# Macaron layer (FFN, retention, FFN) on eight cores: VectorE's start written as alternating chains, first FFN of chunk 5 ahead of V 0, second FFN of chunk 8 held back to the end, Wo 2 and a second FFN exchanged in step 4

## What is computed

```python
def _L0_ffn_ref(x, weight, bias):            # weights and rows in blocks of 32
    xq, xs = _mx_quantize(x2)                # fp6 grid, scale = max|block| / 7.5
    wq, ws = _mx_quantize(w2)
    out = (xq * xs[..., None]) @ (wq * ws[..., None]).T + bias
def _retention(X, Wq, Wk, Wv):               # 8 heads of 128
    scores = jnp.einsum('bhnd,bhmd->bhnm', q, k) / np.sqrt(DH)
    ret = jnp.einsum('bhnm,bhmd->bhnd', scores * decay[None], v)
    ret = (ret - mean) * jax.lax.rsqrt(var + EPS)        # per head
# attention: silu(X @ W_G) * Y @ W_O, with X 2048 x 1024 on each core
x = x + 0.5 * _L0_ffn_ref(_layernorm(x), weight, bias)
x = x + _L0_attn_ref(_layernorm(x), Wq, Wk, Wv, W_G, W_O)
x = x + 0.5 * _L0_ffn_ref(_layernorm(x), weight, bias)
```

## Time and profile before

| | us |
|---|---|
| median of 3 runs (lowest, highest) | 485.18 (484.07, 485.69) |
| the profiled execution | 484.67 |
| span of its slowest core, from first to last instruction | 482.8 |
| spans of the eight cores | 479.5 to 482.8 |
| TensorE busy in the span | 432.3 (90%) |
| VectorE busy | 342.6 (71%) |
| GpSimd busy | 256.4 (53%) |
| ScalarE busy | 190.5 (39%) |

### The profile page before, as it was taken

The page is one execution under the profiler, slowest core; times in us unless marked ns, Lnnn a source line. Parts: engine busy times, 40 slices in busy tenths (PEclk is TensorE's granted clock), DMA queues, the critical chain, the costliest instruction groups (busy, mean ns, idle before and its releaser), DMA issues.

```text
span 482.8 us, 8182 instructions; the slowest of 8 cores (479.5 to 482.8 us)
## 1 busy us (share of the span) xinstructions
PE 432.3 (90%) x2410; PEld 215.5 (45%) x2456; DVE 342.6 (71%) x656; ACT 190.5 (39%) x270; POOL 256.4 (53%) x328
## 2 busy tenths in 40 slices
PE   0226799999998999999999999999999999999894
PEld 0113354545543535454545445454545454555442
DVE  3886866477888859687786868586947466756782
ACT  1547265236442071607061533426152534614400
POOL 0888765325477554655647464647451624436243
PEclk9999899999999999999999999999999999999999
DMA  7999999974363393635343533645340524233143
GB/s 200 309 182 182 189 157 183 155 116 87 89 110 67 94 208 92 110 67 143 75 133 67 153 68 88 88 88 88 87 81 12 107 45 85 47 67 65 44 153 131
DMA packets 99451, 54.47 MB, mean 113 GB/s; under 512 B 88784, under 2 KB 89040, under 8 KB 99408
## 3 DMA queue, kind: packets, MB, share of 16 engines
q1 hardware_dynamic: 93984, 43.43, 39.5%
q0 software_dynamic: 5280, 10.49, 14.9%
q10 hardware_dynamic: 144, 0.03, 0.0%
HBM read 34.28 MB, written 8.39 MB: 88 GB/s over the span
## 4 chain that ended last, share of the span: by engine, by line
PE 72%; DVE 12%; issue 6%; ACT 3%; DMA 3%; POOL 2%; SPq 1%; DVEq 1%; ACTq 0%; POOLq 0%
PE p L818 64%; DVE p L419 2%; DVE arena L434 2%; PE p L928 2%; DMA arena<-arena 2%; PE pstate L908 1%; PE p L859 1%; DVE arena L444 1%; DMA arena<-wf 1%; PE p L863 1%; PE p L847 1%; ACT arena L709 1%; ACT arena L681 1%; PE pstate L872 1%; DVE arena L522 1%
## 5 line engine op out<-in xcount | busy, mean ns | idle before, releaser
L818 PE MATMUL p<-arena 128*128 128x512 bf16 x1715 | 383.2, 379 | 8.1 <-ACT arena L709 2.7
L818 PEld LDWEIGHTS p<-arena 128*128 128x128 bf16 x1760 | 169.6, 98 | 206.8 <-issue 10.6
L434 DVE BATCH_NORM_STATS2 arena<-arena 128x6 f32<-128x512 f32 x96 | 66.5, 692 | 9.9 <-DVE arena L436 2.2
L669 ACT ACTIVATE arena<-arena 128x1024 bf16<-128x1024 f32 x16 | 19.9, 1243 | 129.1 <-POOL arena L1072 129.1
L1112 POOL TENSOR_TENSOR arena<-arena 128x1024 bf16<-128x1024 fp8e4 x16 | 34.3, 2144 | 46.9 <-DVE arena L449 46.9
L681 ACT ACTIVATE arena<-p,arena 128x128 bf16<-128x128 f32 x128 | 46.4, 473 | 19.2 <-POOL arena L1085 19.2
L444 DVE TENSOR_REDUCE arena<-arena 128x32 f32<-128x1024 f32 x29 | 35.3, 1216 | 19.3 <-ACT arena L660 10.8
L513 DVE TENSOR_TENSOR arena<-p,arena 128x1024 bf16<-128x1024 f32 x16 | 19.6, 1223 | 41.0 <-PE p L818 40.5
L908 PE MATMUL pstate<-arena 128*128 128x128 bf16 x168 | 16.4, 261 | 34.3 <-POOL arena L1048 27.5
L1105 POOL TENSOR_TENSOR arena<-arena 128x1024 bf16<-128x1024 fp8e4 x16 | 30.5, 1909 | 29.3 <-DVE arena L449 26.3
L449 DVE SCALAR_TENSOR_TENSOR arena<-arena 128x1024 fp8e4<-128x1024 f32 x29 | 37.3, 1285 | 3.4 <-DVE arena L448 0.5
(11 more groups left out here) (52 smaller groups left out, 397.1 us busy)
## 6 DMA issues: line engine op xcount, KB each, us to landing
arena<-x SPq DMA_DIRECT2D x16, 512.0 KB, 5.3
out<-arena SPq DMA_DIRECT2D x16, 512.0 KB, 2.8
arena<-wf SPq DMA_DIRECT2D x8, 512.0 KB, 11.5
arena<-wk POOLq DMA_DIRECT2D x2, 1024.0 KB, 19.9
arena<-wq POOLq DMA_DIRECT2D x2, 1024.0 KB, 31.5
arena<-wg POOLq DMA_DIRECT2D x2, 1024.0 KB, 40.0
arena<-wv POOLq DMA_DIRECT2D x2, 1024.0 KB, 41.2
arena<-wo POOLq DMA_DIRECT2D x2, 1024.0 KB, 34.0
```

What stands on the lines that cost most here:

```text
L434: step(e.bn_stats(bn_ln[:, n, 6 * half:6 * half + 6], x[:, 512 * half:512 * half + 512]))
L818: last = e.matmul(pair[:, half * 512:half * 512 + 512], lhs[:, kc, :], w[:, kc, half * 512:half * 512 + 512], start=(kc == 0), stop=(kc == ...
```

## The change

VectorE's first instructions are written as two chains that alternate: while one weight block or chunk waits for its own last result, an instruction of the next stands between. ScalarE loads its function table at once (`warm`) and takes some steps in another order; GpSimd issues four of its loads later and takes its small steps in another order. On TensorE `f1(5)` is taken ahead of `proj(0, "v")` instead of behind `ret(0)`; the first FFN of chunk 1 is cut in two halves; `proj(2, "v")` and `wo(0)` are exchanged; in step 4 `wo(2)` and `f2(1)` are exchanged. `f2(8)` leaves step 11 and joins the units behind `sc(15)`, where two units (chunks 11 and 14) are also cut in halves around a turn. The x loads of chunks 6 and 7 go behind `kt(1)`, `qt(1)` and the arrival of Wv.

```diff
-F2_IN = 9
+F2_IN = 8
...
-             ("g", 1, 1), ("v", 0, 0), ("sc", 0, 1), ("v", 1, 2), ("ret", 0, 1),
-             ("f1", 5, 0), ("k", 2, 2), ("q", 2, 0), ("sc", 1, 1), ("g", 2, 2),
-             ("ret", 1, 1), ("wo", 0, 0), ("v", 2, 2),
+             ("g", 1, 1), ("f1", 5, 0), ("v", 0, 2), ("sc", 0, 1), ("v", 1, 0),
+             ("ret", 0, 1), ("k", 2, 2), ("q", 2, 0), ("sc", 1, 1), ("g", 2, 2),
+             ("ret", 1, 1), ("v", 2, 0), ("wo", 0, 2),
...
+        if F2_IN + 3 <= i < LATE:
...
+        elif i == STEADY:
+            order += [("f1", i + 3, 0), ("sc", i - 1, 1), ("wo", i - 2, 2),
+                      ("ret", i - 1, 1), ("f2", i - 3, 0), ("k", i, 2), ("q", i, 0),
+                      ("g", i, 2), ("v", i, 1)]
...
-    late_home = {9: cols(o_xc1[0]), 10: cols(o_xc1[0] + 2048), 11: cols(o_xc1[1]),
+    late_home = {8: cols(o_xd1[0]), 9: cols(o_xc1[0]), 10: cols(o_xc1[0] + 2048), 11: cols(o_xc1[1]),
...
+            elif c == 8:
+                e.wait_ge(sem["tr_x10"], 16 * n_dma(14, X1_DMA, 2))
...
-        e.wait_ge(sem["t_k"], 2)
+        kt(1)
+        qt(1)
+        e.wait_ge(sem["ld_wv"], 32)
         x_first(6)
-        kt(1)
         x_first(7)
...
+        store(8)
...
+        def w_max(j):
             e.wait_ge(sem["ld_wf%d" % j], 16)
+            own.up(e.tensor_reduce(w_amax[j % 4].unsqueeze(2), b32(wst_sb[j]), AX, ALU.max,
+                                   apply_absolute_value=True))
+            at["w_max", j] = own.n
+        def w_scale(j):
             if j >= 4:
                 e.wait_ge(sem["g_wd"], j - 3)
+            e.wait_ge(sem["v_self"], at["w_max", j])
+            own.up(e.tensor_scalar(w_scl[j % 4], w_amax[j % 4], 0.5 * R7_5, 0.5 * FLOOR,
+                                   ALU.mult, ALU.max))
+            at["w_scale", j] = own.n
+        def w_recip(j):
+            e.wait_ge(sem["v_self"], at["w_scale", j])
+            own.up(e.reciprocal(w_rs[j % 4], w_scl[j % 4]))
+            at["w_recip", j] = own.n
+        def w_mul(j):
             if j >= 2:
                 e.wait_ge(sem["s_wy8"], j - 1)
+            e.wait_ge(sem["v_self"], at["w_recip", j])
+            e.scalar_tensor_tensor(b32(wy_sb[j % 2]), b32(wst_sb[j]), 0.5,
+                                   bc32(w_rs[j % 4]), ALU.mult, ALU.mult
+                                   ).then_inc(sem["v_wy"], 1)
...
-        wquant(0)
-        wquant(1)
-        st1(0)
-        for j in range(2, 6):
-            wquant(j)
-        q1(0)
-        wquant(6)
-        st1(1)
-        wquant(7)
-        q1(1)
-        st1(2)
-        q1(2)
+        w_max(0)
+        w_scale(0)
+        w_max(1)
+        w_recip(0)
+        w_scale(1)
+        w_mul(0)
+        x_st(0, 0)
+        w_recip(1)
+        x_st(0, 1)
+        w_mul(1)
+        w_max(2)
+        x_mean(0)
+        w_scale(2)
+        for j in range(3, 6):
+            w_max(j)
+            w_recip(j - 1)
+            w_scale(j)
+            w_mul(j - 1)
+        x_max(0)
+        w_recip(5)
+        x_scale(0)
+        w_mul(5)
+        w_max(6)
+        x_recip(0)
+        w_scale(6)
+        x_mul(0)
+        x_st(1, 0)
+        w_recip(6)
+        x_st(1, 1)
+        w_mul(6)
+        w_max(7)
+        x_mean(1)
+        w_scale(7)
+        x_st(2, 0)
+        w_recip(7)
+        w_mul(7)
+        x_max(1)
+        x_st(2, 1)
+        x_scale(1)
+        x_mean(2)
+        x_recip(1)
+        x_mul(1)
+        x_max(2)
+        x_scale(2)
+        x_recip(2)
+        x_mul(2)
...
         evV(3)
         ev2(0)
         st2(4)
-        for i in range(STEADY, NC):
+        mask(3)
+        ev1(7)
+        q1(8)
+        evO(2)
+        gn(3)
+        ev2(1)
+        st2(5)
+        st3(2)
+        st1(9)
+        q2(2)
+        zmul(3)
+        evV(4)
+        q1(9)
+        for i in range(STEADY + 1, NC):
...
-        for j in range(KC - 1):
+        e.wait_ge(sem["g_const"], 2)
+        e.activation(warm, nhalf, AF.Identity, bias=ntie)
+        wy8(0)
+        wy8(1)
+        xc1(0)
+        for j in range(2, 6):
             wy8(j)
-            if 2 <= j:
-                wcp(j - 2)
-            if j == 2:
-                xc1(0)
-            if j == 4:
-                e.wait_ge(sem["ld_bias"], 16)
-                e.activation(bias_sb, bias_sb, AF.Identity, scale=0.5
-                             ).then_inc(sem["s_bias"], 1)
-        xc1(1)
+            wcp(j - 2)
+        e.wait_ge(sem["ld_bias"], 16)
+        e.activation(bias_sb, bias_sb, AF.Identity, scale=0.5).then_inc(sem["s_bias"], 1)
+        wcp(4)
+        wy8(6)
         wcp(5)
         xcp(0)
+        xc1(1)
         wy8(7)
         wcp(6)
+        xc1(2)
         wcp(7)
-        xc1(2)
         xcp(1)
         xcp(2)
         tn(0)
...
         tn(4)
         for i in range(STEADY, NC):
             if i < LATE:
-                tn(i + 1)
+                if i > STEADY:
+                    tn(i + 1)
                 scopy(i - 1)
                 evK(i)
+                if i == STEADY:
+                    tn(i + 1)
                 xc2(i - 2)
...
+        def f2_half(c, half):
+            e.wait_ge(sem["tr_x2"], 16 * (c + 1))
+            pair = emptied("f2", c)
+            for kc in range(KC):
+                last = e.matmul(pair[:, half * 512:half * 512 + 512], xdt2_at(c)[:, kc, :],
+                                wdt_sb[:, kc, half * 512:half * 512 + 512],
+                                start=(kc == 0), stop=(kc == KC - 1),
+                                skip_group_check=True)
+            if half == 1:
+                last.then_inc(sem["t_f2"], 1)
...
-        f1(1)
+        f1_half(1, 0)
         xtr(2)
+        f1_half(1, 1)
         f1_half(2, 0)
...
+        xtr(5)
         proj(1, "g")
-        xtr(5)
         e.wait_ge(sem["s_t"], 3)
         turn("t2", t_sb)
+        f1(5)
         proj(0, "v")
         sc(0)
         proj(1, "v")
         ret(0)
-        f1(5)
         proj(2, "k")
         proj(2, "q")
         sc(1)
         proj(2, "g")
         ret(1)
+        proj(2, "v")
         wo(0)
-        proj(2, "v")
...
             if i < LATE:
                 f1(i + 3)
                 sc(i - 1)
-                if i < F2_IN + 3:
+                if STEADY < i < F2_IN + 3:
                     f2(i - 3)
                 else:
                     wo(i - 2)
                 ret(i - 1)
-                if i < F2_IN + 3:
+                if i == STEADY:
+                    f2(i - 3)
+                elif i < F2_IN + 3:
                     wo(i - 2)
                 proj(i, "k")
             else:
...
-        f2(9)
+        f2(8)
         ret(NC - 1)
         wo(NC - 2)
+        f2(9)
         f2(10)
-        f2(11)
         e.wait_ge(sem["s_Sc"], NC - 1)
         e.wait_ge(sem["v_z"], NC)
         turn("z%d" % Z_PE, z_sb)
+        f2_half(11, 0)
         wo(NC - 1)
+        f2_half(11, 1)
         f2(12)
         f2(13)
-        f2(14)
+        f2_half(14, 0)
         e.wait_ge(sem["g_xd2"], NC)
         turn("y%d" % X2_PE, xd2_sb)
+        f2_half(14, 1)
         f2(NC - 1)
...
-        cast_load("wg", 1)
         xd1(0)
         b1(0)
         wd(6)
-        cast_load("wv", 0)
         sm1(1)
         wd(7)
         xd1(1)
         sm1(2)
+        cast_load("wg", 1)
+        cast_load("wv", 0)
+        xd1(2)
         b1(1)
+        sm2(0)
         cast_load("wv", 1)
-        xd1(2)
-        sm2(0)
         b1(2)
         sm1(3)
         sm2(1)
+        xd1(3)
         cast_load("wo", 0)
-        xd1(3)
+        b1(3)
         cast_load("wo", 1)
-        b1(3)
         sm1(4)
         sm2(2)
+        sm1(5)
         b1(4)
         xd1(4)
-        sm1(5)
         b1(5)
         xd1(5)
...
```

More of the change, by code:

```diff
@@ L180, in build_program @@
     y82_sb = f8at(take(1024), D)
-    xd1_sb = [bfat(take(2048), D) for _ in range(2)]
+    o_xd1 = [take(2048) for _ in range(2)]
+    xd1_sb = [bfat(o, D) for o in o_xd1]
     o_xd2 = take(2048)
@@ new lines, in x_recip, with x_mul, x_st @@
+        def x_recip(c):
+            e.wait_ge(sem["v_self"], at["x_scale", c])
+            own.up(e.reciprocal(x_rs[c], q1_scl[c % 2]))
+            at["x_recip", c] = own.n
+        def x_mul(c):
+            e.wait_ge(sem["v_self"], at["x_recip", c])
+            e.scalar_tensor_tensor(b32(y81_sb[c % 2]), b32(xc1_sb[c % 2]),
+                                   sm[:, 0, c, 2:3], bc32(x_rs[c]), ALU.mult, ALU.mult,
+                                   saturate=False).then_inc(sem["v_q1"], 1)
+        def x_st(c, half):
+            if c >= 1 and half == 0:
+                e.wait_ge(sem["v_st1"], c)
+            e.wait_ge(sem["ld_x%d" % c], 16)
+            own.up(e.bn_stats(bn_ln[:, 0, 6 * half:6 * half + 6],
+                              x_sb[c][:, 512 * half:512 * half + 512]))
+            at["x_st", c] = own.n
@@ L554, in prog_vector @@
         st1(4)
+        st1(5)
         q1(4)
         ev1(3)
-        st1(5)
         q1(5)
         ev1(4)
+        ev1(5)
         evV(0)
@@ L565, in prog_vector @@
```

(2 more changed lines are left out.)

77 lines of the change are left out of this document (36 added, 41 removed).

## The result

The changed kernel takes **490.0 us** in the median (489.38 to 491.32, 4 runs), the kernel before 484.91 on the same chip: a ratio of 1.010, 95% interval 1.0078 to 1.0121. I had forecast 481.0, and 485.0 as the upper end.

The account below looks back on a forecast made before the run. TensorE's matmuls bound the long middle, so only the start, some waiting steps and the end could give time. Core 2's terms summed to -4.25 us; slowest core 4 fell 4.15, giving a median of 481.0, range 477.5 to 485.0.

Parts of the forecast that it names:

- VectorE's chains: Start: alternating instructions on VectorE bring the first FFN of chunk 2 earlier, -4.9 us (bounds 0 and -5.5).
- the rule of the Trainium skill: VectorE empties before each instruction anyway, so alternating saves nothing: 485.5; with a half effect, 483.5; chance of either 0.14.
- The new waits: Start: TensorE waits 0.95 and 0.7 for normalized rows of chunks 0 and 1, +1.65 us (bounds 0 and 3).
- Clock: Start, core 2 alone: half a unit fills a wait and the clock holds, -1.3 us (bound 0).
- Behind retention 0: Retention 0 to 1: scores 1 need norm 0, G 2 needs evK 2; of 3.45 removed only 0.45 returns, +3.0 us.
- R: The start of retention 0 in the forecast, 98.9 us; retention 1 was to start at R + 14.75.
- The x load: Behind retention 0: chunk 6's load goes out at R + 1.9, takes 5.2, and costs 0.3 us.
- rival 4: Behind retention 0: chunk 6's load lands late and the kernel gets slower, up to 492.4 us; chance 0.12.
- Step 4: Steps 4 and 5: exchanging Wo 2 and second FFN 1 removes 2.2 of 3.9 waiting, -1.7 us (bounds 0 and -3.9).
- End: Last turns: half units cover two copy waits (-2.7), but xd2(15) comes later; -1.1 us (bounds +0.5 and -2.7).
- the sum for core 2: All terms on core 2: -4.9 - 1.3 + 1.65 + 3.1 - 1.7 - 1.1 = -4.25 us, span 482.8 to 478.55.
- The rivals: Alternating saves nothing or half (0.14), start's gain passes whole, 477.1 (0.16), chunk 6's load late and slower (0.12).

Follow-up runs that it names:

- e6: Changed kernel with only the x loads of chunks 6 and 7 back ahead of the transposes of K 1 and Q 1: 489.26 us, ratio 1.0094.
- e12: Kernel before with only first FFN 5, its PSUM pair and its eviction moved in front of V 0: 490.58 us, ratio 1.0130.
- e10: e7 with first FFN 5, its PSUM pair and eviction in front of V 0, as in the changed kernel: 488.3 us, ratio 1.0072.
- e7: e5 with the fourth step exchanged (new start, early x loads, first FFN 5 behind retention 0, old end): 484.03 us, ratio 0.9972.
- e3: Changed kernel with Wo 2 and second FFN 1 back in the old order of the fourth step, all engines: 490.05 us, ratio 1.0109.
- e5: e4 with the x loads of chunks 6 and 7 back at their old place: 483.7 us, ratio 0.9984.
- e9: e7 with the changed end (second FFN 8 held back, halves around the last turns): 485.03 us, ratio 1.0004.
- e11: e7 with the second half of second FFN 11 moved behind the turn of z 15: 483.29 us, ratio 0.9973.
- e2: Changed kernel with second FFN 8 back in its own step and no halves around the last turns: 487.81 us, ratio 1.0061.
- e4: Changed kernel with first FFN 5 behind retention 0, the old end and the old fourth step put back; x loads still late: 487.21 us, ratio 1.0056.

## Why the forecast was wrong, step by step

In short, three terms failed beyond their size. The end was to win 1.1 and lost 2.2, because taking second FFN 8 out of step 11 was put at nothing and cost 1.9. The exchange in step 4 was to win 1.7 and only moved the waits. And the clock was to win 1.3 on core 2, where the new waits brought new low stretches. The move of first FFN 5 had the right mechanism and nearly the right price, but a gain at the start of 2.15 did not cover it.

- **VectorE's chains (-4.9):** right at the source (34.85 for a forecast of 34.9; a block saves 0.52). By the rule of the Trainium skill that I had set against it (VectorE: DVE Perf Modes, The DRAIN you can't avoid) alternating would have saved nothing; the trace disagrees, by these numbers. The same section adds that a next instruction that isn't held starts earlier, and that the trace bears out: the maximum starts at 18.48, while the product in front of it ends at 18.56. On TensorE the first FFN of chunk 2 came at 52.1, not 51.4. The new waits were 1.95, not 1.65, and one of 0.44 follows at 77.89, also for GpSimd.
- **Clock (-1.3): the wrong sign.** I let one low stretch vanish and asked of none of the new waits whether it would bring another. On core 2 three came: around 44, 112 and 187 us, where 16 matmuls took 4.51, 4.93 and 5.22 in place of 3.6: 0.9, 1.3 and 1.6 lost. And core 2 was a poor sample: only three cores had a low stretch to win back before. The start's gain, 3.1 there for a forecast of 4.55, is 2.15 in the mean of the cores.
- **Behind retention 0 (+3.0):** the mechanism was seen rightly (the wait for norm 0, then for evK 2, and "Of 3.45 us of work taken away only 0.45 comes back"; retention 1 at R + 16.2 for R + 14.75, the difference being the low clock), but taken for the price of a gain and not for a reason against the move. The size was good too: with the clock kept and the load early the stretch takes 14.87 (e6, e12) for 15.65, with 3.46 less in it, 2.7 lost. e10 and e12 show the whole move alone: +4.3 and +6.0. My excuse for it, that V 0 would otherwise wait 2.1 for Wv, was void: in e7 V 0 waits 0.23 for Wv on core 5 and nothing on the other seven. I had carried over the landing at 89.8, though the change issues other loads around it; in the profile after, Wv had landed at 87.
- **The x load (0.3 of the +3.0; rival 4, 0.12):** issued at R + 2.0 and landed after 5.1, both as forecast. As a longer wait ahead of G 2 it cost 0.4 in the mean of the cores (e6), near the forecast. Whether it also brought more low clock isn't shown.
- **Step 4 (-1.7):** the exchange saves at most 0.8 of the stretch (e3) and nothing between e5 and e7. f2(1) and G 4 lost their waits as forecast, and V 4 waits 1.06 for my 1.35, but f2(2), which I let wait 0.7, waits 1.75. In the kernels with the exchange it mostly waits 0.8 to 2.2, in those without it mostly under 0.6. And one wait was not in the sum at all: first FFN 7 for its transpose, 1.0 (last section).
- **End (-1.1):** +2.2. This is the term that failed most. I counted second FFN 8 as neutral, since the number of units stays. But the steps without a second FFN have no work to cover the other engines with, and one more step is now like that: 1.9 lost between update 10 and scores 15 (e9: 1.5), seen as waits of 0.48 for evQ in step 11 and, on most cores, of 0.2 to 0.9 for DMA in step 14 or at scores 15. The part that I had worked out came out well: from scores 15 on 0.77 is won with the clock kept, for 1.1. The halves took the copies' waits away and gave 1.98 at xd2(15), where I had 1.6. But behind the 1.98 five cores fell to the low clock, 1.7 each. One half alone saves 0.1 (e11).

Against the sum for core 2, -4.25, the means show by the same steps: start -2.15 for -4.55 (-3.25 on the five cores that had the full clock already), behind retention 0 +4.4 for +3.0, steps 2 to 4 +0.8 for -1.6, end +2.2 for -1.1. All four missed to the same side. The rivals were built around the start and the load; none said that moving a filler out costs more than the start gives, though the +3.0 was on the page.

**Left open.** Why the step from update 11 to 12 takes 22.9 in e2, e4, e5, e7, e10 and e11, and 22.5 in the kernel before and in the changed one; in e7 TensorE waits 0.22 for evQ there on every core, before it doesn't. That 1 to 4 is 0.7 longer with the new start (e5) though all its work is the same goes back, by the traces, to one instruction of VectorE (last section); no experiment was made on it. The clock was read, not changed by an experiment, and what decides whether a core falls to the lower level behind a wait stays open.

## What to carry to other kernels

- A unit of matmuls that can run at any time is worth most where it covers other engines' chains. Before moving one, write down what it covers; if the sum says "the work taken out doesn't come back as time", that is an argument against the move by itself.
- A load put behind a transpose in an in-order queue inherits that transpose's wait. Check when it is issued, and what stands behind its first user on that engine: here an eviction, and behind it a PSUM pair.
- Judge an edit on all cores and from each core's own start, and try it alone: the parts here, +4.3 for first FFN 5, +1.0 to 1.8 for the end and 0.4 or more for the load, against 2.2 of gain, were hidden in one number.
